# The causal mask of an attention block moved from TensorE to a GpSimd select (plain fp32 products)

## What is computed

```python
q = (x @ wq).reshape(B, T, 2, 4, 128)              # 8 heads, 2 key heads
k = einsum('bkhl,ld->bkhd', k_lat, wk_up)          # k_lat, v_lat: 32 wide
scores = einsum('bqhrd,bkhd->bhrqk', q, k) * 128 ** -0.5
scores = where(tril(ones((T, T))), scores, finfo.min)
probs = softmax(scores, axis=-1)
y = einsum('bhrqk,bkhd->bqhrd', probs, v) @ wo
```

## Time and profile before

| what | us |
|---|---|
| median of 3 runs | 678.4 (676.56 to 681.41) |
| the profiled execution, its own time | 677.78 |
| span from its first to its last instruction | 676.0 |
| TensorE busy | 553.4 (82%) |
| VectorE busy | 406.7 (60%) |
| ScalarE busy | 355.1 (53%) |
| GpSimd busy | 153.3 (23%) |

### The profile page before, as it was taken

The page is one execution under the profiler, slowest core; times in us unless marked ns, Lnnn a source line. Parts: engine busy times, 40 slices in busy tenths (PEclk is TensorE's granted clock), DMA queues, the critical chain, the costliest instruction groups (busy, mean ns, idle before and its releaser), DMA issues.

```text
span 676.0 us, 10472 instructions
## 1 busy us (share of the span) xinstructions
PE 553.4 (82%) x3342; PEld 240.0 (36%) x3342; DVE 406.7 (60%) x1500; ACT 355.1 (53%) x841; POOL 153.3 (23%) x257
## 2 busy tenths in 40 slices
PE   3825687898989889989889779988899789899836
PEld 2512234243432343334424433334334332333332
DVE  4343576777665675865667475865756756473225
ACT  2232254367555744757657444748556554476612
POOL 2130410034100102531004302511025110143213
PEclk9957779699999997999999979999999987999958
DMA  4002001000111000001101000001101000000000
GB/s 130 0 16 58 18 24 36 2 12 6 40 46 27 25 2 0 17 19 45 43 8 29 13 16 2 1 12 46 36 3 41 16 3 0 1 17 16 17 0 16
DMA packets 23816, 14.56 MB, mean 22 GB/s; under 512 B 5640, under 2 KB 23632, under 8 KB 23760
## 3 DMA queue, kind: packets, MB, share of 16 engines
q1 hardware_dynamic: 23184, 13.49, 7.3%
q10 hardware_dynamic: 576, 0.39, 0.2%
HBM read 3.78 MB, written 2.10 MB: 9 GB/s over the span
## 4 chain that ended last, share of the span: by engine, by line
PE 55%; DVE 17%; ACT 10%; issue 7%; POOL 4%; SPq 4%; ACTq 1%; DMA 1%; POOLq 0%; DVEq 0%
PE bank L1088 13%; PE bank L1157 10%; PE bank L1160 8%; PE bank L1138 7%; PE bank L1125 6%; SPq L505 3%; DVE masked L899 3%; ACT scaled L657 3%; ACT prob L699 3%; DVE m_part L902 2%; PE bank L1080 2%; ACT xn L632 2%; DVE dve_sum L872 2%; PE bank L1171 2%; DVE bank L824 2%
## 5 line engine op out<-in xcount | busy, mean ns | idle before, releaser
L699 ACT ACTIVATE prob<-bank,exp_scale 128x512 f32<-128x512 f32 (+3 forms) x384 | 214.3, 583 | 202.3 <-PE bank L1141 146.5
L899 DVE CUSTOM_DVE_ANT_0 masked<-bank,mask_qk 128x128 f32<-128x128 f32 (+3 forms) x256 | 122.4, 485 | 111.2 <-PE bank L1125 110.0
L1125 PE MATMUL bank<-k_stack,q_stack 96*128 96x512 f16 (+3 forms) x384 | 132.2, 349 | 37.3 <-DVE m_part L902 11.0
L1088 PE MATMUL bank<-we,xT 128*128 128x512 f32 x256 | 143.8, 657 | 20.6 <-ACT scaled L657 15.7
L1138 PE MATMUL bank<-q_stack,k_stack 98*128 98x512 f16 (+3 forms) x384 | 128.7, 342 | 7.3 <-ACT prob L699 5.4
L902 DVE TENSOR_REDUCE m_part<-bank 128x1 f32<-128x512 f32 x128 | 87.4, 683 | 38.5 <-PE bank L1125 38.0
L573 POOL TENSOR_TENSOR pair_sum<-dve_sum,scaled 128x256 f32<-128x256 f32 x64 | 46.6, 728 | 255.4 <-DVE dve_sum L872 215.9
L1157 PE MATMUL bank<-prob,v_lat 128*32 128x512 f32 (+3 forms) x768 | 86.6, 524 | 0.5 <-ACT prob L699 0.5
L657 ACT ACTIVATE scaled<-bank,gate 128x128 f32<-128x128 f32 x256 | 72.7, 373 | 24.6 <-PE bank L1088 11.4
L1160 PE MATMUL bank<-prob,ones 128*32 128x512 f32 (+3 forms) x768 | 84.0, 510 | 0.0
L1138 PEld LDWEIGHTS bank<-q_stack,k_stack 98*128 98x128 f16 x384 | 39.4, 103 | 92.7 <-issue 48.2
(11 more groups left out here) (106 smaller groups left out, 502.9 us busy)
## 6 DMA issues: line engine op xcount, KB each, us to landing
q_stack<-q_hi SPq DMA_DIRECT2D x120, 32.0 KB, 1.8
x<-in_L_attn_x SPq DMA_DIRECT2D x8, 256.0 KB, 2.8
out_x<-x SPq DMA_DIRECT2D x8, 256.0 KB, 2.3
q_stack<-q_lo SPq DMA_DIRECT2D x60, 32.0 KB, 1.9
k_stack<-k_hi SPq DMA_DIRECT2D x32, 32.0 KB, 1.8
we<-in_L_ffn_expert_weights SPq DMA_DIRECT2D x1, 512.0 KB, 4.2
x<-in_L_attn_wq SPq DMA_DIRECT2D x1, 512.0 KB, 6.0
x<-in_L_attn_wo SPq DMA_DIRECT2D x1, 512.0 KB, 7.2
```

Source lines behind the costliest of these rows:

```text
L699: nc.scalar.activation(into, bank[ST + n % NST][:, 0:w], ACT.Exp, scale=exp_scale[:, 0:1]).then_inc(p_ready, 1)
L899: V.tensor_tensor_reduce(out=masked[:, m % 2, 0:w], in0=seen, in1=mask_qk[:, CH - w:CH], op0=ALU.add, op1=ALU.max, scale=1.0, scalar=LOWES ...
L1088: mm(take_fb(("y", f, n, j))[:], x_part(2 * f, n, t * P, (t + 1) * P), we[:, cols(half)], start=True, stop=True).then_inc(y_done, 1)
L1125: mm(into[:, 0:w], q_stack[0:MROW, c, g * NR + r, (i % TC) * P:(i % TC + 1) * P], k_stack[0:MROW, b % 2, g, k:k + w], start=True, stop=Tru ...
```

## The change

The mask matmul goes. The exponentials are taken of unmasked scores, and GpSimd then zeroes in `prob` those of later keys, with one `affine_select` for each diagonal group over the 4 heads' squares (128 partitions x 4 x 128), in place. `weighted_values` of a diagonal group waits for the select (`p_kept`) in place of the exponential, and stands one slot later; so do what follows a quad's end, the joins, and the last unit of the FFN. The two constants of the mask matmul go too.

```diff
-PV_LAG = 3
+PV_LAG = 4
...
-CONST_STEPS = 9
+CONST_STEPS = 5
...
-    + [... Unit(1, NB, NN - 1, 1, NALL + 11, QUICK)]
+    + [... Unit(1, NB, NN - 1, 1, NALL + 12, QUICK)]
...
 def join_slot(n):
     b, c = divmod(n, NC)
-    return b * NS + (47, 103)[c]
+    return b * NS + (48, 104)[c]
...
             step(nc.gpsimd.memset(half_power[:], -0.5))
-            step(nc.gpsimd.memset(ident_b[:], 0.0))
-            select(ident_b[:], 0, [[-1, P]], 1)
             step(nc.gpsimd.memset(mask_qk[:], 0.0))
             select(mask_qk[:, CH - P:CH], 0, [[-1, P]], 1, ALU.is_ge, MASKED)
-            step(nc.gpsimd.memset(mask_kq[:], 0.0))
-            select(mask_kq[:], 0, [[1, P]], -1, ALU.is_ge, MASKED)
...
+            def keep_causal(b, q, j):
+                pool.wait_ge(p_ready, group_end(b, q, j) + 1)
+                square = prob[:, GROUP[b, q, j] % NPG, :, 0:P]
+                nc.gpsimd.affine_select(out=square, in_=square, compare_op=ALU.is_ge, fill=0.0, base=0,
+                                        pattern=[[0, NR], [1, P]], channel_multiplier=-1).then_inc(p_kept, 1)
...
             for s in range(LO, HI):
+                if s - 1 + PV_LAG in PV_AT and on_diagonal(*PV_AT[s - 1 + PV_LAG][1:]):
+                    keep_causal(*PV_AT[s - 1 + PV_LAG])
                 if s - 2 in END_AT:
                     normalise(END_AT[s - 2])
...
-                last = mm(into[:, 0:CH - off], k_stack[:, b % 2, g, j * P:(j + 1) * P],
-                          q_stack[:, c, g * NR + r, off:CH], start=True, stop=not on_diagonal(q, j))
-                if on_diagonal(q, j):
-                    last = mm(into[:, 0:P], ident_b[:], mask_kq[:], start=False, stop=True)
-                last.then_inc(st_done, 1)
+                mm(into[:, 0:CH - off], k_stack[:, b % 2, g, j * P:(j + 1) * P],
+                   q_stack[:, c, g * NR + r, off:CH], start=True, stop=True).then_inc(st_done, 1)
...
-                pe.wait_ge(p_ready, group_end(b, q, j) + 1)
+                if on_diagonal(q, j):
+                    pe.wait_ge(p_kept, DIAGONAL[b, q, j] + 1)
+                else:
+                    pe.wait_ge(p_ready, group_end(b, q, j) + 1)
```

More of the change, by code:

```diff
@@ L71 @@
 BACK = [Unit(1, b, b * NC, NC, (b + 1) * NS + (48 if b < NB - 2 else 14), WIDE) for b in range(NB - 1)] \
-    + [Unit(1, NB - 1, NN - 2, 1, NALL - NS + 60, QUICK), Unit(1, NB, NN - 1, 1, NALL + 11, QUICK)]
+    + [Unit(1, NB - 1, NN - 2, 1, NALL - NS + 60, QUICK), Unit(1, NB, NN - 1, 1, NALL + 12, QUICK)]
 UNITS = sorted(FRONT + BACK, key=lambda u: u.start + u.pace.y)
@@ L76 @@
 TILE = {k: i for i, k in enumerate(TILES)}
-LO, HI = -72, NALL + 48
+LO, HI = -72, NALL + 49
 def join_slot(n):
     b, c = divmod(n, NC)
-    return b * NS + (47, 103)[c]
+    return b * NS + (48, 104)[c]
 def tile_slot(f, n, t):
@@ L174 @@
 GROUP = {g: i for i, g in enumerate(GROUPS)}
+DIAGONAL = {g: i for i, g in enumerate(g for g in GROUPS if on_diagonal(*g[1:]))}
 def first_query(q, j):
@@ L292, in macaron @@
         ident = sb("ident", [P, P])
-        ident_b = sb("ident_b", [P, P], BF16)
         mask_qk = sb("mask_qk", [P, CH])
         masked = sb("masked", [P, 2, CH])
-        mask_kq = sb("mask_kq", [P, P], BF16)
         ones = sb("ones", [P, DL])
@@ L411, in macaron @@
         p_ready = sem("p_ready")
+        p_kept = sem("p_kept")
         pv_done = sem("pv_done")
```

## The result

The changed kernel is slower, by 1%: ratio of after to before 1.0099 [1.0073, 1.0125], medians 684.63 and 676.56 us over 17 runs each. The prediction was 672.4 us, in a range of 665 to 680: wrong in direction, and outside its range.

What follows compares the result with a forecast made beforehand. Bound mostly by TensorE's in-order stream, in places by VectorE and the score-exponential loop. Removal -6.2, waits +0.2, collisions +0.5, earlier scores -0.5: -6.0 us, from 677.78 to 671.8 profiled, median about 672.4; range 665 to 680.

Steps and rivals of the forecast that it cites:

- The moved values product: TensorE's values product one slot later: gives nothing by itself, only the fillers sharing its slot change; -2 to +2 us, taken 0.
- The removal: 256 mask matmuls leave TensorE's stream: 8.2 us on the path, three quarters kept, -6.2 us.
- The count of pieces: Mask matmul pieces in the chain of what ended last: 130 of nearly always 0.06 us, together 8.2 us.
- rival C: Gain taken back by the next chain or by TensorE longer at 1.2 GHz: -3 to +3 us, chance 0.20.
- Rival B: Mask matmuls on TensorE worth more than their steps: -9 to -14 us, middle -11, 667 us, chance 0.12.
- back-to-back issue gap: Skill's rule for TensorE matmuls among weight loads: 81 ns each, making the 130 mask pieces an estimated 10.5 us.
- The select: 64 selects on GpSimd, 0.9 us each, between 0.62 and 1.27; 58 us more busy time there.
- Waits for it: TensorE's values products waiting for GpSimd's select: one of 63 diagonal groups short, 0.2 us.
- Rival D: TensorE waits for GpSimd's select: sign turns from about 2.2 us a select, 688 us at 3 us, chance 0.08.
- Collisions on GpSimd: Select delaying older work in GpSimd's queue, such as additions: three places found, 0 to 2 us, taken 0.5.
- The end: Last group's uncovered select, paid for by the values product's later place: -0.1 to +1 us, taken 0.
- What would show it: Signs: selects of 0.6 to 1.3 us, ScalarE's wait some 190 us; wrong if the clock fell in new places.

Runs made afterwards that it cites:

- e2: Kernel before without its 256 mask matmuls and nothing in their place, values product still 3 slots behind: 0.9953, 673.8 us.
- e11: Kernel before, mask kept, with the values product 4 slots behind instead of 3, joins and last FFN unit unmoved: 1.004, 678.6 us.
- e5: Kernel before without mask matmuls and without select, values product 4 slots behind, joins as before: 1.0034, 679.3 us.
- e3: Kernel before, mask kept, with values product, joins and last FFN unit each one slot later: 1.017, 687.3 us.
- e12: Kernel before, mask kept, with only the joins and last FFN unit one slot later: 1.0017, 677.3 us.
- e15: Kernel before, mask kept, joins later, only the 64 diagonal values products one slot later: 0.998, resting on 4 of 11 executions; median of all 687.34 us.
- e1: The changed kernel run again for a profile, against the kernel before: 1.0107, 683.0 us.
- e13: Changed kernel with joins and last FFN unit back in their old places, against the kernel before: 1.0044, 680.2 us.
- e14: Changed kernel with only the 64 diagonal values products later, the other 32 groups 3 slots behind, against the kernel before: 1.0018, 678.6 us.
- e16: Changed kernel with only diagonal values products later and joins back in place, against the kernel before: 0.9972, 675.7 us.
- e17: Kernel before with the select added beside its mask matmuls, values product 3 slots behind: 1.0061, 682.6 us.

## Why the prediction was wrong, step by step

**The step that failed** is "The moved values product": "What changes is which fillers (expert products, projections) share its slot: I count 37 such slots before and 38 after. From -2 to +2 us, taken 0", and with it "The joins move along; [...] No cost seen". Together they cost 1.017 [1.0135, 1.0205], 11 us; alone they cost 1.004 and 1.0017, of which the joins' 1.0017 cannot be told from 1. I counted how many fillers share a slot with the product, not which wait it had covered. Even the count misled: by the plan in the two kernels 37 and 38 take in transposes, router and joins; with expert products or projections alone it is 26 slots before and 32 after, the six new ones with query projections. "It waited for nothing before" was true and beside the point: others waited behind it. That the joins' bank is shared was noticed, and VectorE's addition, which frees it, not traced to its next user (3.0 us in three places).

**The removal, -6.2 us**: too much, 3.2 at lag 3 (e2) and about 0 at lag 4 (e11 to e5). The count of pieces (8.2 us, 8.0 from unrounded times) is not contradicted: with the clock's part added back by the estimate, e2 comes to 6.7 to 9.1 us. What took the gain is what rival C named, in both its halves: VectorE steps in (its pieces in the chain grow by 6.2 us in e2), and TensorE is at 1.2 GHz for 13 us longer. How the loss divides between them is not shown. I had given C as a whole 0.20, and made of its clock a single stretch of up to 5 us. Rival B (worth more than its steps) falls: no run without the mask gained more than 0.5%, and over all 256 masks of before's trace the next matmul starts 0.059 us behind the mask in the median. With it falls the estimate from the Trainium skill's back-to-back issue gap of 81 ns ("TensorE: Matmul & The Clock Gate").

**The select, 0.9 us each**: mis-sized but harmless. It took 0.635 us, at the lower bound of 0.62, the slope of the memset, and not at the select's own row of 128 columns taken four times.

**Waits for it, 0.2 us**: near, 0.4, and 1.0 of the weight loads. The list of times to spare held. Rival D, which would have turned the sign from 2.2 us a select, was excluded by GpSimd's rows, and rightly.

**Collisions on GpSimd, 0.5 us**: nothing found against it. VectorE's statistics wait 26.1 us for `finish_tile`, 26.6 before. GpSimd's addition takes 726 ns, 728 before, and all 64 selects 631 to 642 ns. It is small steps of VectorE that are held up. Of after:

```profile
364.73 0.63 POOL L583 TENSOR_SCALAR_AFFINE_SELECT prob<-prob 128x512 f32<-128x512 f32 x1
364.84 0.54 DVE L794 TENSOR_TENSOR diff<-diff 128x8 f32<-128x8 f32 x1
```

The step, a square, has both inputs in SBUF and takes 0.17 us in the median; here it ends within 0.02 us of the select. Three steps end so with a select, 1.0 us over their medians together; with all of GpSimd's work it is 14 steps and 3.5 us after, 14 and 4.1 before. So the trace agrees with the rule of the shared port pair in the Trainium skill ("SBUF — State Buffer"), at about the microsecond that I had estimated, and it is no part of the loss.

**The end, 0**: right. Of after, in the order of the timeline:

```profile
648.87 0.64 PE L1164 MATMUL bank<-prob,v_lat 128*32 128x256 f32 x8
...
649.41 0.63 POOL L583 TENSOR_SCALAR_AFFINE_SELECT prob<-prob 128x512 f32<-128x512 f32 x1 [2.07 <-ACT prob L706]
...
650.10 0.43 PE L1164 MATMUL bank<-prob,v_lat 128*32 128x128 f32 x8 [0.16 <-POOL prob L583]
```

The select runs beside the product of the group before it, and the last product waits 0.16 us; compare.

**What would show it**: ScalarE's wait went to the scores, 223.5 us and not the 190 forecast, as the idle of before under other names and the 8 us of longer span joined it. "If the clock fell in new places" was the right alarm. There was none for waits between instructions that the diff does not touch.

**What stays open.** Product and joins together cost 1.7%, singly 0.4 and 0.2, though their listed waits only add up. The sum of time at 1.2 GHz does not explain it: 108 us in e3, 103 in e11, 111 in e12 and before. By the estimate of 0.27 to 0.45 us each, e11's 8 us less hide 2 to 4 us of loss, and 5 to 6 of e3's 11 us are still left. It could be where the stretches at 1.2 GHz fall, as e15 and e11 have two courses 10 to 12 us apart without a change in the program, but no run separates the stalls from these stretches. For the same reason the loss has no single division: taken as order first, it is +1.7% (e3) and -0.6% for removal with select (e1 against e3); with the joins in their old places it is +0.4% (e11) and 0.0% (e13 against e11).

## What to carry to other kernels

Before an instruction is moved in an in-order stream, list what it stood in front of: which later instructions of that engine need a bank that another engine is still to free, and how much time the moved piece had given them. Then do the same for everything that shares its constant or its place in the plan (here the joins). Move only what needs to move: the later place for diagonal groups alone, with the joins left, turned 1.0107 into 0.9972. And where TensorE waits at times and its clock varies, don't price removed matmuls at their steps: here 256 of them were worth 3 us of 15 one way, and 1 us of 15 the other.

## What was not expected of the hardware

The granted clock went with the amount of small matmul work: time at 1.2 GHz was 124 us with none of the mask matmuls, 111 with them and 89 with twice as many, at lag 3 throughout, and times of 673.8, 676.6 and 678.0. It is a tendency and not a law (of those without them e14 has 111 and e16 115; e17, with them and the select, has 117).

One execution of the changed kernel took 2452.73 us. Its groups, where the clock is shown as 1.0 throughout:

```profile
L1095 PE MATMUL bank<-we,xT 128*128 128x512 f32 x256 | 645.2, 2714 | 1.4 <-ACT scaled L664 1.4
...
L583 POOL TENSOR_SCALAR_AFFINE_SELECT prob<-prob 128x512 f32<-128x512 f32 x64 | 40.8, 637 | 877.8 <-ACT prob L706 877.8
```

An expert product took 2714 ns where it takes 655, and the select 637 as ever. It came once in some 190 executions of these kernels, and its cause is not known.
